# Attention inside the experts stage, and a combining round that starts with the result

## What is computed

```python
# attention of layer 0 (16 heads of 16); k, v likewise from x
q = elu(x @ w_q.T) + 1.0
kv = einsum('bnhd,bnhm->bhdm', k, v)
z = 1.0 / (einsum('bnhd,bhd->bnh', q, k.sum(axis=1)) + 1e-06)
out = einsum('bnhd,bhdm,bnh->bnhm', q, kv, z).reshape(b, n, d)
attn = out @ w_out.T + b_out
# experts of layer 0: each token goes to 2 of 16
out_e = lmlp(xt, W1[e], b1[e], W3[e], b3[e], W2[e], b2[e])   # silu(x W1) * (x W3), then W2; each with a "time" column
y = lresnet(y, out_e, weight)          # for each expert that was hit: z = y + w*out, then z / sqrt(time^2 - space^2)
y = lresnet(y, lmlp_shared(xt), 1.0)
```

## Time and profile before

| | us |
|---|---|
| median of 3 runs (1770.51 to 1777.24) | 1770.83 |
| span of the profiled execution | 1773.8 |
| stretch of the experts stage, 373 to 606 | 233 |
| stretch of attention and combining, 606 to 929 | 323 |
| all other stages | 1217.8 |

### The profile page before, as it was taken

One profiled execution on the slowest core, in us unless ns is written; L12 is line 12 of the kernel. 1 busy time (PEld: TensorE's weight loads), 2 busy tenths in 40 slices (PEclk: granted clock), 3 DMA queues, 4 the chain that ended last, 5 costly groups with the idle time before them and its releaser, 6 DMA issues. The chain is left out here.

```text
span 1773.8 us, 63284 instructions
## 1 busy us (share of the span) xinstructions
PE 1368.2 (77%) x21833; PEld 947.5 (53%) x21834; DVE 1388.7 (78%) x3576; ACT 1252.4 (71%) x3382; POOL 1218.6 (69%) x1312
## 2 busy tenths in 40 slices
PE   3549999969899736455534899999997799999857
PEld 2515555545555425344422566666664566666646
DVE  7878877856566479988846999999984688888748
ACT  7818888846666568778837888888753677777745
POOL 6738888733233488777615899999974677787747
PEclk9999999989999977777767999999998999999969
DMA  8627787769999657766643566665643122222239
GB/s 259 226 94 183 206 198 196 198 156 211 206 219 220 183 158 177 199 162 169 167 113 89 115 125 128 126 129 118 123 102 77 45 53 53 52 52 52 53 97 290
DMA packets 495359, 256.31 MB, mean 145 GB/s; under 512 B 359357, under 2 KB 484864, under 8 KB 494720
## 3 DMA queue, kind: packets, MB, share of 16 engines
q1 hardware_dynamic: 482658, 219.11, 51.0%
q0 software_dynamic: 12576, 35.67, 6.7%
HBM read 79.52 MB, written 73.44 MB: 86 GB/s over the span
## 5 line engine op out<-in xcount | busy, mean ns | idle before, releaser
L213 PE MATMUL ps<-all_late,l_xq_T 128*128 128x352 f16 x1536 | 252.5, 316 | 57.3 <-DMA l_xq_T<-l_apart 30.7
L213 PEld LDWEIGHTS ps<-all_late,l_xq_T 128*128 (+1 forms) x1536 | 146.9, 99 | 149.4 <-DVE ffn_h L711 45.9
L213 PE MATMUL ps<-l0moe_W,all_xT_all 128*128 128x16 f16 (+2 forms) x1152 | 190.6, 312 | 32.0 <-ACT all_xT_all L912 22.3
L1455 POOL TENSOR_TENSOR all_late<-experts_se,all_mhalf 128x4 f32<-128x4 f32 (+1 forms) x77 | 76.4, 993 | 159.9 <-DVE experts_se L1564 145.4
L2308 POOL TENSOR_TENSOR all_late<-ret_pm,all_late 128x512 f16<-128x512 f32 x128 | 145.5, 1158 | 20.8 <-ACT all_late L2214 20.8
L213 PEld LDWEIGHTS ps<-l0moe_W,all_xT_all 128*128 128x128 f16 x1152 | 83.6, 100 | 117.0 <-ACT all_xT_all L912 26.0
L619 PE MATMUL ps<-all_late,ffn_hT 128*128 128x256 f16 x1088 | 131.9, 276 | 9.3 <-ACT l_xq_T L683 5.8
L1720 PE MATMUL ps<-l_kvm,both_q 128*128 128x136 f16 x384 | 38.3, 269 | 122.5 <-DVE both_o L1893 112.1
L213 PE MATMUL ps<-moe_E,experts_gT 128*128 x864 | 117.4, 276 | 15.4 <-DMA experts_gT<-slots_dram 10.6
L619 PEld LDWEIGHTS ps<-all_late,ffn_hT 128*128 128x128 f16 x1088 | 106.8, 99 | 29.8 <-issue 8.0
L364 POOL TENSOR_TENSOR ffn_h<-ffn_fq_val,ffn_h 128x704 f16<-128x704 f32 x64 | 97.5, 1523 | 14.9 <-ACT ffn_h L359 14.9
(11 more groups left out here) (301 smaller groups left out, 4697.2 us busy)
## 6 DMA issues: line engine op xcount, KB each, us to landing
rows_dram<-all_late SPq DMA_DIRECT2D x72, 256.0 KB
ret_v<-ret_vpad SPq DMA_DIRECT2D x256, 64.0 KB
front_xin<-x SPq DMA_DIRECT2D x16, 512.0 KB, 4.3
x_dram<-front_x SPq DMA_DIRECT2D x16, 512.0 KB, 5.0
all_late<-x_dram SPq DMA_DIRECT2D x64, 128.0 KB
z_dram<-all_late SPq DMA_DIRECT2D x64, 128.0 KB
both_zin<-z_dram SPq DMA_DIRECT2D x16, 512.0 KB
both_xin<-x SPq DMA_DIRECT2D x16, 512.0 KB
```

The source lines that it names most:

```text
L213: mm = pe.matmul(out, lhs[a], rhs[b], start=first and n == 0, stop=last and n == 2, skip_group_check=True)
L1455: pool.tensor_tensor(rows[:, n % 4, which, :, 0], se[:, u, which], power[:, which], ALU.pow).then_inc(s_time, 1)
```

## The change

Everything of attention but the last product (`output`) moves from the last stage into the experts stage, as further entries of each engine's list. `each_pair` runs a stage at every second step, with half the step's number as the pair of token tiles. Two pairs of expert tiles go with one pair of token tiles. POOL does the low part of the attention's result (`attended_lo`, before: `out_lo`) behind `times(n)` of every even n from 8 on, for pair (n - 8)/2. SP gets `turn_attended`, skew 10, behind `store` of the same step; it waits for ACT's and POOL's halves, and turns them into the place of the input's transpose, `xT_all`. Buffers of attention are laid into weights and sums that the stage no longer needs. The last stage, now `phase_combine`, keeps `output` of attention, which waits for no DMA any more, and DVE's round there has a new order.

```diff
+def each_pair(stage):
+    def run(t):
+        if t.slot4 % 2 == 0:
+            stage(Tile(t.n // 2, t.slot4 // 2 % LAG, t.n // 4))
...
@@ SP of phase_experts
-            unrolled(count, [(7, turn_hidden), (0, turn_rows), (11, store)])
+            def turn_attended(t):
+                p = t.n // 2
+                if t.n < TILES and t.n % 2 == 0:
+                    sp.wait_ge(s_ohi, p + LAG + 1)
+                    sp.wait_ge(s_olo, p + LAG + 1)
+                    sp.dma_start_transpose(xT_all[:, t.n:t.n + U].rearrange("p k c m -> p (k c) m"),
+                                           o16[:, p % LAG].rearrange("p k a d -> p (k a d)")).then_inc(s_oT[p % LAG], 16)
+            unrolled(count, [(7, turn_hidden), (0, turn_rows), (11, store), (10, turn_attended)])
@@ POOL of phase_experts
+            def attended_lo(p):
+                pool.wait_ge(s_ohi, p + LAG + 1)
+                pool.tensor_tensor(o16[:, p % LAG, :, 1], o[:, p % LAG], o16[:, p % LAG, :, 0], ALU.subtract).then_inc(s_olo, 1)
...
             for n in range(count + OLAG):
                 times(n)
+                if n % 2 == 0 and 0 <= n - 8 < TILES:
+                    attended_lo((n - 8) // 2)
@@ PE, ACT and DVE of phase_experts
-            pipeline(pe, count, [(EXPERT_LAG, experts_both), (0, experts_first), (EXPERT_LAG, down), (0, project)], 12)
+            scheduled(pe, [(EXPERT_LAG, count, experts_both), (0, count, experts_first), (EXPERT_LAG, count, down),
+                           (0, TILES, queries), (5, TILES, each_pair(numerators)), (0, count, project)], 12, 12, 4)
...
-            pipeline(act, count, [(7, output), (3, hidden_hi), (1, gate)], 4)
+            scheduled(act, [(7, count, output), (3, count, hidden_hi), (1, count, gate), (3, TILES, each_pair(query_hi)),
+                            (8, TILES, each_pair(attended_hi)), (1, TILES, each_pair(negative))], 4, 12, 13)
...
-            pipeline(dve, count, [(7, out_clamp),
-                                  (2, square),
-                                  (2, hidden_clamp),
-                                  (3, hidden_lo),
-                                  (1, hidden)], 4)
+            scheduled(dve, [(7, count, out_clamp),
+                            (2, count, square),
+                            (2, count, hidden_clamp),
+                            (2, TILES, each_pair(query)),
+                            (3, count, hidden_lo),
+                            (1, count, hidden),
+                            (3, TILES, each_pair(query_lo)),
+                            (6, TILES, each_pair(divide))], 4, 12, 13)
@@ PE of phase_combine
-            stages = [(8, output), (4, numerators), (0, queries)]
+            stages = [(6, output)]
@@ DVE of phase_combine, each round
             for i in rounds:
+                if group(i - 4):
+                    result(group(i - 4), 0)
+                    result(group(i - 4), 1)
+                    add_input(group(i - 4))
                 if group(i - 2):
                     second(group(i - 2), i)
                 if group(i - 3):
                     third(group(i - 3), i)
-                attend(2 * i, stages)
-                if group(i - 4):
-                    result(group(i - 4), 0)
                 if group(i - 1):
                     first(group(i - 1), i)
                 if group(i - 2) or group(i - 3):
                     inner(i)
-                attend(2 * i + 1, stages)
-                if group(i - 4):
-                    result(group(i - 4), 1)
-                    add_input(group(i - 4))
```

More of the change, by code:

```diff
@@ L146, in pipeline, with scheduled, step @@
         step(None, s)
+def scheduled(eng, stages, slots, first, passes):
+    def step(c, i=None):
+        for skew, count, stage in stages:
+            k = c - skew
+            if i is not None:
+                stage(Tile(slots * i + k, k % LAG, slots // LAG * i + k // LAG, k % slots))
+            elif 0 <= k < count:
+                stage(Tile(k, k % LAG, k // LAG, k % slots))
+    for c in range(first):
+        step(c)
+    with eng.Fori(0, passes) as i:
+        for r in range(slots):
+            step(first + r, i)
+    for c in range(first + slots * passes, max(skew + count for skew, count, _ in stages)):
+        step(c)
 def unrolled(count, stages, slots=LAG):
@@ new lines, in numerators @@
+            def numerators(p):
+                if isinstance(p.n, int) and p.n == 0:
+                    pe.wait_ge(s_step, BATCH * C + 2)
+                pe.wait_ge(s_qlo, done(p))
+                pe.wait_ge(s_qhi, done(p))
+                pe.wait_ge(s_o, prev(p))
+                for k in range(U):
+                    for c in range(C):
+                        kv = [kvm16[:, bass.ds(p.n // (TB // U), 1), part, c].rearrange("p o k -> p (o k)")
+                              for part in range(2)]
+                        for n, (a, b) in enumerate(((0, 0), (1, 0), (0, 1))):
+                            ins = pe.matmul(nps[:, k, c], q16[:, p.slot, a, c, k * P:(k + 1) * P], kv[b],
+                                            start=c == 0 and n == 0, stop=n == 2, skip_group_check=True)
+                ins.then_inc(s_num, 1)
@@ L1698, in _ @@
         def _(pe):
[L1699 to L1713, removed]
-                pe.wait_ge(s_qhi, done(t))
-                pe.wait_ge(s_o, prev(t))
-                for k in range(U):
-                    for c in range(C):
-                        kv = [kvm16[:, t.n // (TB // U), part, c] for part in range(2)]
-                        for n, (a, b) in enumerate(((0, 0), (1, 0), (0, 1))):
-                            ins = pe.matmul(nps[:, k, c], q16[:, t.slot, a, c, k * P:(k + 1) * P], kv[b],
-                                            start=c == 0 and n == 0, stop=n == 2, skip_group_check=True)
-                ins.then_inc(s_num, 1)
+            prime(pe, s_out)
             def output(t):
-                pe.wait_ge(s_oT[t.slot], landed(t))
                 if t.n >= OUTS:
@@ L1843, in combine @@
                     squares(group(i - 3), 2, i)
-            upper = [(6, out_hi), (3, query_hi)]
             for i in rounds:
```

186 lines of the change are left out of this document (93 added, 93 removed).

## The result

The changed kernel takes **2040.0 us** (median of 4 runs, 2038.0 to 2044.1) against 1773.7 for the kernel before (4 runs, 1770.5 to 1777.2): ratio 1.151, 95% interval 1.148 to 1.154. The prediction was 2080, range 1990 to 2150. The profiled execution has a span of 2042.3 us (1773.8 before).

A forecast was written before the change was run, and what follows sets the result against it. It took a new dependence through ACT, DVE, POOL, SP and DMA to bound the experts stage at 17.6 us per pair instead of 6.22: 1773.8 + 370 - 59 = 2085, less 3, rounded to 2080 us, range 1990 to 2150.

The forecast's parts named there:

- SP and DMA: Experts stage, per pair of steps: attention's transpose issued in 1.68, 0.07 between, hidden layer's transpose to its matmul 2.69; 4.44 us.
- PE: Experts stage, per pair: twenty matmuls of `down` and `queries` at the lower clock, 4.4, then `project` 1.80; 6.2 us.
- ACT: Experts stage, per pair: `gate` about 0.4, `query_hi` 0.62, the two instructions of `negative` 0.58 and 0.72; 2.3 us.
- output to power: Experts stage, per pair: `output`, `out_clamp`, `hidden_clamp` and the power, from ACT's copy to the power's end; 3.4 us.
- The way into it: Experts stage, ahead of the 31 pairs: four `queries` and three `numerators`, 8.5 us, and the dependence's first round, 8.4 us.
- Combining: Last stage without attention: 264 us instead of 323, so -59, with 15 rounds of 14.0.
- the other bound: Last stage: L1750 beside the sums is gone; if it held one up each round, 18 us more, 77 given back.
- the chain: Last stage, loop from norm to norm through gate, results, input row, sums, squares and power: 14.0 us a round, above POOL's 13.5.
- the order's price: Last stage: with sums ahead of the result as before, `gate` would hide; the new order costs about 0.5 us a round.
- the dependence doesn't reach PE: Rival, experts stage: POOL's half is ready when SP comes, PE bounds at 8.2 us per pair; 1785 us, 7%.
- faster: Rival: PE bounds, `numerators` and part of `queries` hide in its gaps, 7.7 us per pair, combining gives 77; 1750 us, 4%.
- The clock stays up: Rival, experts stage: PE's gap is shorter or its clock level returns within `down`, 15.8 us per pair; 2025 us, 17%.

The follow-up runs named there:

- experiments 1 to 3: Changed kernel with SP's issue of attended rows at 14 instead of 10, at 12, or with POOL's subtraction ahead of its power: 1759.9, 1764.4, 1843.2 us.
- experiment 7: Kernel before, attention left in place, with POOL's subtraction for the attended rows' lower half moved to VectorE: 1749.2 us, ratio 0.987.
- Experiment 6: Changed kernel with SP's issue of attended rows at 14 instead of 10, and VectorE's combining round in the old order: 1751.9 us, ratio 0.989.
- experiment 1: Changed kernel with SP's issue of attended rows 14 steps behind instead of 10: 1759.9 us, ratio 0.994.
- experiment 5: Changed kernel with 60 overwritten filler matmuls ahead of `down` in every even step but those of the first twelve steps: 2021.2 us, ratio 1.141.

## Why the prediction was right

It held the time and the sign; the mechanism stood as told, step by step, and experiments 1 to 3 show it by taking it apart. What would show it, did: SP released by POOL (9.6 us of idling, 8 expected), PE idle 7.7, released by `experts_hT`, clock 0.72 (0.75).

The terms of the pair, predicted and as the rows above have them: SP and DMA 4.44, measured 4.11 (573.80 to 577.91; the issue took its lower bound, 1.24, not 1.68); PE 6.2, measured 6.23; ACT 2.3, measured 2.08; output to power 3.4, measured 3.58; the subtraction 1.3, measured 1.19. Sum 17.6, measured 17.19. Over the 31 pairs from `down(4)` (407.74) to `down(66)` (927.04) it is 16.75, since the last pairs, with no more `queries` in them, take 14 to 16: 326 more than before where I had 353. The way into it was 10 us longer than before, not 17. So the 370 came out as 340: the terms that were too large are, in the main, the issue's time (0.3 us a pair), the four pairs at the end that I priced as full (some 10 us), and the way into the loop (7 us).

Combining was sized at -59 and gave -72. One round, from the power's start at 1067.80 to the next at 1080.59, 12.8 where I had added up 14.0 (the 14 rounds with gathers take 12.1 to 13.6, 13.0 on average):

```profile
1067.80 2.31 POOL L1868 TENSOR_TENSOR both_norm<-both_diff,both_power 128x12 f32<-128x12 f32 x1
1070.14 1.70 ACT L1902 ACTIVATE both_y<-both_y,both_norm 128x256 f32<-128x256 f32 x4 [0.28 <-POOL both_norm L1868]
...
1071.88 1.29 DVE L1973 SCALAR_TENSOR_TENSOR both_y<-ps,both_y 128x512 f32<-128x512 f32 x2 [1.99 <-ACT both_y L1902]
...
1073.20 1.22 DVE L1979 TENSOR_TENSOR both_y<-both_y,both_xin 128x1024 f32<-128x1024 f32 x1
...
1074.53 1.67 DVE L1953 SCALAR_TENSOR_TENSOR both_y<-both_y,both_weight,both_ob 128x256 f32<-128x256 f32 x4
...
1076.35 1.67 DVE L1965 SCALAR_TENSOR_TENSOR both_y<-both_y,both_norm,both_zin 128x256 f32<-128x256 f32 x4
...
1079.62 0.95 POOL L1848 DMA_INDIRECT both_ob<-rows_dram,moe_pos_hi  x1 [0.30 <-issue]
...
1080.59 2.93 POOL L1868 TENSOR_TENSOR both_norm<-both_diff,both_power 128x12 f32<-128x12 f32 x1
```

The gate, the results, the input row and the sums stand in one line, as predicted. But the two sums take 1.67 each, not 2.3, and the input row 1.22, not 1.6: I had taken means of the kernel before that held POOL's subtraction in them. That is the step that failed, a term sized too large by 1.7 us a round. I had the other bound in hand (77) and the Trainium skill's rule for it, in the section named in experiment 7, and kept the mean of the rows instead; experiment 7 shows that the subtraction decides here. The power went the other way: my 2.1 was a mean over three sizes, and the one with 12 columns takes 2.3, or 2.9 in six rounds.

With that the chain isn't the longer one any more, which I had said it would be. VectorE's last instruction ahead of the power ends at 1080.26, 12.5 behind the power before; POOL's last gather ends at 1080.57, and the power starts at 1080.59. The rounds with gathers are POOL's, and only the last three are the chain's.

So the order's price was right by luck. I had 0.5 us a round because the chain would be longer than POOL's round by that much, 8 us in 16 rounds. Experiment 6 measured 8 us, 7 of them in combining, but these come from three rounds at the end (12.7 us) less a gain in the 14 before (5.6).

How the 72 divide: the subtraction alone is worth some 20 (experiment 7), the order costs 7 of the stage (experiment 6). The rest, some 59, is by argument the work of VectorE and ScalarE that went with attention; no run takes that apart.

Of the rivals, *the dependence doesn't reach PE* was priced at 1785 and experiment 1, which makes it true, measured 1760: its pair was 7.89, not 8.2, and combining gave more. The point from which *faster* decides, 8.1 us a pair, is bracketed: at 7.97 the kernel is 6 us faster than before, at 10.4 it is 72 slower. Worked back from these two over 31 pairs it lies at 8.1 to 8.2, an estimate. *The clock stays up* didn't come about (0.72, and `queries` took 2.75 to 2.77 in all 27 pairs that have them); its price of 1.8 us a pair is what experiment 5's pairs at 15.2 show.

## What to carry to other kernels

Before an issue is put into a queue, follow what it waits for back through every engine's order, and count how many steps lie between that and the first instruction behind it in the queue that the next step needs: here that was the step just done, and two steps more of skew removed 276 us. Work that is moved to where engines are idle pays only as long as the stage that takes it grows by less than the other one gives back; here all of it together, with the issue at 13 and the old order, gave 1.7%, and one subtraction moved to VectorE in the kernel before gave 1.3% (experiment 7). A right total can stand on a wrong place: the order's 8 us were right in the sum and lay in other rounds than I had said. And a mean duration that lies a fifth above the median can be another engine's doing: look for the longest ones and what they end with before using it in a sum.

## What the hardware showed that I hadn't expected

- The price of an exclusion is on the small instructions too: four columns took 1617 ns in place of 166. It goes both ways. In experiment 6 a gather that POOL issues in 0.95 took 1.69 while VectorE added the input row (two inputs in SBUF), and was done 0.8 after it:

```profile
782.47 0.95 POOL L1848 DMA_INDIRECT both_y<-rows_dram,moe_pos_lo  x1 [0.30 <-issue]
783.36 1.22 DVE L1979 TENSOR_TENSOR both_y<-both_y,both_xin 128x1024 f32<-128x1024 f32 x1
783.72 1.69 POOL L1848 DMA_INDIRECT both_y<-rows_dram,moe_pos_lo  x1 [0.30 <-issue]
```

- POOL's power is held up at its start, and doesn't hold VectorE up behind it. In the changed kernel six of the 14 powers of 12 columns took 2.9 to 3.0 in place of 2.3. In each an instruction of VectorE with two inputs in SBUF had begun 0.10 to 0.13 ahead of the power; those that began later, while it ran, kept their 0.89:

```profile
1080.47 0.89 DVE L368 SCALAR_TENSOR_TENSOR both_fq_val<-both_fq_big,both_fq_val 128x704 f32<-128x704 bf16 x1 [0.21 <-ACT both_fq_big L363]
1080.59 2.93 POOL L1868 TENSOR_TENSOR both_norm<-both_diff,both_power 128x12 f32<-128x12 f32 x1
1081.39 0.89 DVE L374 SCALAR_TENSOR_TENSOR both_fq_val<-both_fq_big,both_fq_val 128x704 f32<-128x704 bf16 x1
1082.32 0.89 DVE L382 TENSOR_TENSOR both_fq_val<-both_fq_val,both_fq_step 128x704 f32<-128x704 f32 x1
```

  In the kernel before, L1880 began while a power ran six times and took 0.68 each time. So for the power the exclusion doesn't last for the whole instruction. What sets the power apart from the subtraction, which does hold VectorE up, no run here settles.
- The power's time goes with its columns: 1.0 us for 4, 1.7 for 8, 2.3 for 12, where VectorE isn't in its way.
